# Cross-attention and a LoRA feed-forward on one core: the opening, the first scores, the FFN weights and the router's product put in another order and width

## The reference

```
xn  = layernorm(x);  q = xn @ Wq;  k = ctx @ Wk;  v = ctx @ Wv
p   = softmax(q k^T / sqrt(128) + bias, masked)          # 64 x 64 for each batch and head
x1  = x + (p v) @ Wo
x2  = layernorm(x1)
logits = x2 @ router_W^T + router_b (15 columns); the 8 largest probabilities, summed by expert: w
out = x1 + x2 @ base_W^T + base_b + 2 * ((x2 @ A^T) * w) @ B^T     # A: 8 experts x 16 = 128 columns
```

## Time and profile before

| | |
|---|---|
| median of 3 runs | 798.69 us |
| the profiled execution: its time, its span | 798.68 us, 796.9 us |
| TensorE busy | 781.5 us, 98% of the span |
| VectorE, ScalarE, GpSimd busy | 577.1, 335.2, 188.7 us |
| DMA | 118.35 MB, mean 149 GB/s |
| chain that ended last | TensorE 92%, VectorE 4%, ScalarE 2%, issue 2%, DMA 1% |

### The profile page before, as it was taken

One profiled execution on the slowest core, in us unless ns is written; L12 is line 12 of the kernel. 1 busy time (PEld: TensorE's weight loads), 2 busy tenths in 40 slices (PEclk: granted clock), 3 DMA queues, 4 the chain that ended last, 5 costly groups with the idle time before them and its releaser, 6 DMA issues.

```text
span 796.9 us, 16335 instructions
## 1 busy us (share of the span) xinstructions
PE 781.5 (98%) x6366; PEld 653.6 (82%) x6366; DVE 577.1 (72%) x1047; ACT 335.2 (42%) x657; POOL 188.7 (24%) x203
## 2 busy tenths in 40 slices
PE   8899999999999999999999999999999999999998
PEld 7788888888888888778888888887888888888886
DVE  3894526247677666687987798778878888768974
ACT  4553525245555555453433244423433343314420
POOL 0052232114424434242211221222211221010200
PEclk9999999999999999999999999999999999999999
DMA  6436673234454546674563356435553555343002
GB/s 224 146 146 224 205 259 134 105 133 160 159 185 159 172 158 187 213 234 125 160 172 120 108 160 186 121 108 167 164 142 112 145 160 173 101 121 88 0 3 104
DMA packets 108074, 118.35 MB, mean 149 GB/s; under 512 B 44239, under 2 KB 77007, under 8 KB 107998
## 3 DMA queue, kind: packets, MB, share of 16 engines
q1 hardware_dynamic: 107998, 117.31, 47.0%
HBM read 81.64 MB, written 35.65 MB: 147 GB/s over the span
## 4 chain that ended last, share of the span: by engine, by line
PE 92%; DVE 4%; ACT 2%; issue 2%; DMA 1%; SPq 0%; DVEq 0%
PE pY L1378 40%; PE pP L1378 39%; PE pY L1540 4%; PE pO L1565 2%; PE pO L1378 1%; PE pT_ L1565 1%; PE pT_ L1550 1%; PE pS L1550 1%; DMA ctx<-in_ctx 1%; ACT wv_hi L646 1%; DVE y L1096 1%; DVE pr L1135 1%; PE pS L1565 1%; PE pO L1424 1%; DVE sm L1126 0%
## 5 line engine op out<-in xcount | busy, mean ns | idle before, releaser
L1096 DVE TENSOR_TENSOR y<-y,pY 128x512 f32<-128x512 f32 x124 | 84.5, 682 | 19.5 <-PE pY L1378 19.3
L1378 PE MATMUL pY<-wo_hi,oT_hi 128*128 128x512 f32 x248 | 97.2, 392 | 0.7 <-DVE y L1096 0.6
L1378 PE MATMUL pY<-wo_lo,oT_hi 128*128 128x512 f32 x248 | 96.6, 390 | 0.0
L1378 PE MATMUL pY<-wo_hi,oT_lo 128*128 128x512 f32 x248 | 96.5, 389 | 0.0
L1378 PE MATMUL pP<-xo_hi,wk_hi 128*128 128x512 f32 x210 | 83.4, 397 | 0.8 <-ACT v_s L631 0.8
L1378 PE MATMUL pP<-xo_hi,wk_lo 128*128 128x512 f32 x210 | 82.0, 390 | 0.5 <-issue 0.5
L646 ACT CAST wk_hi<-twk 128x256 fp32r<-128x256 f32 x128 | 52.1, 408 | 71.3 <-PE pP L1378 59.9
L1378 PE MATMUL pP<-xo_lo,wk_hi 128*128 128x512 f32 x210 | 81.9, 390 | 0.0
L579 POOL TENSOR_TENSOR bias<-bias,madd 128x512 f32<-128x512 f32 x32 | 43.9, 1382 | 150.3 <-DMA bias<-in_fside_Bx32xSxS 150.3
L885 DVE TENSOR_TENSOR wk_lo<-twk,wk_hi 128x256 fp32r<-128x256 f32 x128 | 58.7, 463 | 22.0 <-ACT wk_hi L646 22.0
L885 DVE TENSOR_TENSOR wk_lo<-wk_raw,wk_hi 128x256 fp32r<-128x256 f32 x96 | 45.7, 476 | 25.6 <-ACT wk_hi L646 25.4
(11 more groups left out here) (277 smaller groups left out, 1912.0 us busy)
## 6 DMA issues: line engine op xcount, KB each, us to landing
v_hbm<-stage SPq DMA_DIRECT2D x64, 256.0 KB, 2.2
k_hbm<-stage SPq DMA_DIRECT2D x64, 256.0 KB, 3.5
k<-k_hbm SPq DMA_DIRECT2D x16, 1024.0 KB, 5.4
v<-v_hbm SPq DMA_DIRECT2D x16, 1024.0 KB, 7.6
wk_raw<-in_L_xattn_Wk SPq DMA_DIRECT2D x16, 512.0 KB, 4.4
wo_raw<-in_L_xattn_Wo SPq DMA_DIRECT2D x16, 512.0 KB, 3.6
bias<-in_fside_Bx32xSxS SPq DMA_DIRECT2D x128, 64.0 KB, 3.5
wk_raw<-in_L_xattn_Wq SPq DMA_DIRECT2D x16, 512.0 KB, 4.6
```

The lines of the kernel that those rows point to most:

```text
L1096: nc.vector.tensor_tensor(y[:, t, :], y[:, t, :], src[:, :], ALU.add).then_inc(y_added, 1)
L1378: mm = nc.tensor.matmul(bank_, a, b, start=first and n == 0, stop=last and n == len(terms) - 1, skip_group_check=read_between)
```

## The change

Nothing is computed in another way; instructions move in the lists of TensorE, ScalarE and VectorE. `warm_up` has 22 transposes instead of 20. The router's product takes GW = 144 columns instead of ARW = 256; the tiles and the zeros in them stay. Hunks 1 and the last are the width; then, by position, ScalarE's opening (line 681), its block 32 (787) and its end (848), VectorE's opening (1008), its loop (1042), block 32 (1159) and end (1261), and TensorE's opening (1466), block 32 (1621), and end (1667).

```diff
@@ -23,6 +23,8 @@
 ARW = 256
+
+GW = 144
 SCALE = float(DH) ** -0.5
@@ -679,22 +681,22 @@
             higher(0, 1)
+            wait_raw(act, 0, (0, 1))
+            nc.scalar.copy(b12[0][:, :, :], raw_block(0, 0, 1)).then_inc(b12_h, 1)
+            higher(0, 5)
             last_high(0)
...
                            ).then_inc(a21_h, 1)
-            wait_raw(act, 0, (0, 1))
-            nc.scalar.copy(b12[0][:, :, :], raw_block(0, 0, 1)).then_inc(b12_h, 1)
             rows_out(1)
...
             copy_p1(1)
-            higher(0, 5)
+            higher(0, 3)
             sums_high(1)
             piece_of_first(2, 4, pP[1], c21_made)
-            higher(0, 3)
+            higher(0, 2)
             piece_of_first(1, 3, pP[0], c12_made)
-            higher(0, 2)
             piece_of_first(3, 7, pP[1], c22_made)
@@ -702,8 +704,8 @@
             copy_p1(2)
+            copy_v(1)
             sums_high(2)
-            copy_v(1)
             higher(0, 6)
@@ -787,10 +789,10 @@
             higher(w, 2)
-            exp(0)
             higher(w, 3)
...
             higher(w, 4)
+            exp(0)
             copy_c12(n)
@@ -848,13 +850,13 @@
             wo_high(NP - 1)
+            split_ffn(4)
             turned_p(h + 2)
             turned_p(h + 3)
-            split_ffn(4)
             split_ffn(5)
+            split_ffn(6)
             o_high(h + 2)
             o_high(h + 3)
-            split_ffn(6)
 
@@ -1008,23 +1010,23 @@
 
+            first_low(0)
             lower_w(0, 0)
-            first_low(0)
             first_low(1)
             lower_w(0, 1)
+            dve.wait_ge(b12_h, 1)
+            lower(b12[1][:, :, :], raw_block(0, 0, 1), b12[0][:, :, :], b12_l)
+            first_t3()
 
...
                   a21_l)
-            dve.wait_ge(b12_h, 1)
-            lower(b12[1][:, :, :], raw_block(0, 0, 1), b12[0][:, :, :], b12_l)
+            first_t2()
+            lower_w(0, 5)
             sums_of_a(1)
-            lower_w(0, 5)
+            lower_w(0, 3)
             sums_low(1)
-            first_t3()
-            first_t2()
-            lower_w(0, 3)
             lower_w(0, 2)
@@ -1042,11 +1044,14 @@
                 w, late, j = next_set(n), late_set(n), prep_at(n)
+                if n < NV:
+                    make_c11(n)
                 if w is not None:
...
                     lower_w(late, 5)
-                make_c11(n)
+                if n >= NV:
+                    make_c11(n)
                 if w is not None:
@@ -1159,23 +1164,23 @@
             lower_w(late, 6)
+            lower_w(w, 2)
+            lower_w(w, 3)
             biased(0)
-            lower_w(w, 2)
+            make_c22(n)
             largest(0)
...
             largest(1)
-            lower_w(w, 3)
             less_max(1)
-            make_c22(n)
             lower_w(w, 4)
-            add_up(0)
             lower_w(w, 5)
...
             n, w2 = QA + 1, next_set(QA + 1)
+            add_up(0)
+            lower_w(w, 6)
             weights(0)
-            lower_w(w, 6)
             lower_w(w2, 0)
@@ -1261,14 +1266,14 @@
             add_tile(i, 6)
+            split_ffn(4)
             add_tile(i, 7)
...
             o_low(h + 2, 1)
-            split_ffn(4)
-            split_ffn(5)
             o_low(h + 3, 0)
             o_low(h + 3, 1)
+            split_ffn(5)
             split_ffn(6)
@@ -1466,9 +1471,8 @@
             turn_ctx(0, first_turn(0))
-            warm_up(4)
+            warm_up(14)
             turn_ctx(1, first_turn(1))
-            warm_up(8)
 
@@ -1621,11 +1625,12 @@
             times(n - 1, 4)
-            times(n, 6)
+            for p in (6, 7, 5):
+                times(n, p)
             scores(0)
             scores(1)
-            for p in (7, 5, 3, 4):
-                times(n, p)
+            times(n, 3)
+            times(n, 4)
             for p in (1, 2, 6, 7, 5, 3, 4):
@@ -1667,13 +1672,14 @@
                 times_wo(i, t)
+                if t == 5:
+                    ffn_weights(4)
             turn_p(h + 2)
             turn_p(h + 3)
-            ffn_weights(4)
             ffn_weights(5)
+            ffn_weights(6)
             times_v(h + 2)
             times_v(h + 3)
-            ffn_weights(6)
 
@@ -1690,8 +1696,8 @@
                     pe.wait_ge(sel_made, E + 1)
-                product(pG[t // 2][:, t % 2 * ARW:(t % 2 + 1) * ARW],
-                        [(xt, (ar[0][:, c, :], ar[1][:, c, :])) for c, xt in enumerate(xt_parts(t))]
+                product(pG[t // 2][:, t % 2 * ARW:t % 2 * ARW + GW],
+                        [(xt, (ar[0][:, c, 0:GW], ar[1][:, c, 0:GW])) for c, xt in enumerate(xt_parts(t))]
                         ).then_inc(g_full, 1)
...
             def base(t):

```

## The result

The changed kernel took **797.17 us** (median of 20 runs, 795.54 to 799.17) against 799.53 us for the kernel before on the same chip (20 runs, 797.39 to 804.88): ratio 0.9968, 95% interval [0.9955, 0.9981], 2.6 us less. Forecast were 794.3 us and 4.4 us less. The profiled executions don't show this: the one after took 799.1 us (span 797.3), the second slowest of its 20, and the one before 798.68 (span 796.9), the seventh fastest of its 20.

A forecast was written before the change was run, and what follows sets the result against it. TensorE, busy 781.5 of 796.9 us, was taken as the bound. Opening -2.7, first scores +0.3, FFN weights -1.0 and router's width -1.0 sum to -4.4: 798.7 to 794.3 us, range 791.2 to 797.5.

The forecast's parts named there:

- The start: TensorE's opening: 14 transposes before context tile 1's turn bring the first product from 9.51 to about 8.5 us, -1.0 us.
- the end of -1.7: Opening: the start's saving if unbroken transposes bring the clock's rise before the first product, instead of -1.0 us.
- B12, B22, T3: Opening: work moved into VectorE's idle time and ScalarE's list ends TensorE's waits at 26.93 and 20.89 us, -1.3 us.
- `copy_v` and the sums: Opening: `copy_v(1)` first shortens the `v_s` wait, -0.7 us; the sums' low part slips, new wait +0.8 us.
- The cover of A21: Opening: A21 ready about 15.2 us, wanted at 15.6, a thin margin; a wait at 15.5 would show the forecast wrong.
- `make_c11`: Opening, VectorE: placed ahead of `lower_w(w, 0)`, the piece no longer stands behind a held-up low part, -0.5 us.
- First scores: Block 32, scores behind product 5: `v_s` wait hidden, -0.93; later pieces +0.8 and +0.5; sum +0.3 us, -0.9 to +0.9.
- FFN weights: End: batch 4 turned after tile 5 ends the `fw_lo` wait, last Wo starts at about 738.05, -1.0 us (-0.3 to -1.3).
- The router's width: Router: 96 matmuls at 144 columns take 0.11 instead of 0.12 us each, -1.0 us.
- The nearest row: Router: transposes of 128 columns, each with its weight load, 0.11 us apart, taken as the narrow matmul's price.
- Rival 1: Router: narrow fp32r product is slow, up to 0.28 us per matmul, +15 us; total 800 to 810 us; chance 0.15.
- Rival 2: VectorE, nearly full in the opening and around 335 to 345 us, takes back TensorE's gain; 796.5 us, chance 0.25.

The follow-up runs named there:

- e3: Kernel before with only batch 4 of the FFN weights turned and split earlier; 797.53 us, ratio 0.9977.
- e4: Kernel before with only the router's product at 144 columns; 799.83 us, ratio 1.0005.
- e14: Changed kernel with 4 transposes instead of 14 between the turns of context tiles 0 and 1; one run, 803.69 us.
- e6: Kernel before with GpSimd's mask addition cut to one element per partition, keys not masked; 796.46 us, ratio 0.9966.
- e9: Changed kernel with copy_c12(32) ahead of exp(0) on ScalarE and add_up(0) behind make_c11(33) on VectorE; 796.79 us, ratio 0.9954.
- e10: Changed kernel with block 32's three stores and a weight load between the two halves of the bias loads in SP's queue; 796.62 us, ratio 0.9960.
- e15: Changed kernel with e9, e10 and add_tile(i, 0) ahead of add_up(h + 3) on VectorE together; 796.04 us, ratio 0.9947.
- e5: Changed kernel with block 32 as before on all three engines, so without the moved scores; 795.27 us, ratio 0.9948.
- e11: Changed kernel with block 32 as before and add_tile(i, 0) ahead of add_up(h + 3) on VectorE; 795.44 us, ratio 0.9947.
- e7: Changed kernel with GpSimd's mask addition cut to one element per partition, keys not masked; 793.72 us, ratio 0.9926.

## Why the forecast was right or wrong

The time fell by 2.6 us where 4.4 were forecast. (The 798.7 from which the forecast subtracts was the median of three runs, 0.8 us below that of twenty.) The same distances in all profiles of these runs, by the old and the new version of each part (mean, lowest to highest):

| stretch | old lists | new lists | forecast |
|---|---|---|---|
| start of the first product | 8.8 (7.7 to 10.1), 6 profiles | 7.7 (7.4 to 8.1), 10 | -1.0 |
| start of the 1345th matmul of 512 columns | 326.1 (323.9 to 328.5), 5 | 322.5 (322.1 to 323.2), 10 | -2.7 |
| from there over the scores to 356 us | 32.23 (32.0 to 32.5), 7 | 33.75 (33.2 to 34.1), 7 | +0.3 |
| attention loop, masks in, `add_up` first | 356.1 (354.4 to 357.1), 4 | 356.7 (355.1 to 358.8), 8 | 0 |
| loop's end to the router (before, e3) | 37.04 | 36.10 | -1.0 |
| router to 787 us (before, e4) | 36.95 | 36.41 | -1.0 |

Their sum is -3.7 + 1.5 + 0.6 - 0.9 - 0.5 = -3.0 us, beside the -2.6 of the ratio. The start stands in the second row too. The ranges of the first scores' row do not touch; those of the loop's do, and its 0.6 can't be told from nothing. By luck the opening gave 1.0 more than its forecast and hid most of the 1.2 that the scores cost beyond theirs.

- **The start (-1.0).** The rise of the clock was assumed to keep its distance to the first product. It came before it: in the changed kernel's profile it is -1.64 at the first matmul of 512 columns and -2.06 at the seventh, near the end of -1.7 that the forecast had kept for this case. The rule of the Trainium skill (TensorE: Matmul & The Clock Gate, Part 4: PE-mode transpose) that transposes don't count is not borne out here: TensorE had done nothing but transposes, and the turn behind the 14 took 0.60 us instead of 1.11 and the first product ran at the high level. With four of them and standstills (e14) the level was lost again after three matmuls.
- **B12, B22, T3 (-1.3), `copy_v` and the sums (-0.7 + 0.8).** As forecast: no wait for `wv_lo` at 25 us; at 31.73 a wait of 0.77 for `v_s` and at 33.89 one of 0.54 behind the sums' low part, which ends at that time. The cover of A21 was as thin as said, and it often failed: in 8 of the 12 profiles with the new lists (not in the changed kernel's own) TensorE waits 0.25 to 0.48 us for it between 14.4 and 15.5 us, which the forecast had named as a sign of being wrong.
- **`make_c11` (-0.5).** -0.4 in the pair of profiles. It is worth more: in two of five profiles with the old order (e4, e6) the wait was 2.03 us, with the new order none was seen. By these rows this and the clock are what makes the opening's mean -3.7 and not the forecast's -2.7.
- **First scores (+0.3): the step that failed.** Its first half held: the wait for `v_s` went, and the two waits came where they were foreseen (`exp` ahead of `copy_c12`, `add_up` ahead of `make_c11`), 0.53 and 0.48 us. Block 32 and 33 take 23.95 instead of 23.36 us, +0.6, inside the forecast's bounds. What the sum lacked is the first pair behind them: from block 33's last product over turns, scores and V it takes 7.34 us on average (6.9 to 7.7) in the seven profiles without the moved scores and 8.31 (7.8 to 8.6) in the seven with them, e9, e10 and e15 left out. Half of the 0.97 stands ahead of the first product with V (0.52 on average), half behind it (0.45). Ahead: SP's queue and one piece of VectorE. Of the queue: eight bias loads, which start when the scores are read, take 5.22 us, the last store of block 32 goes out behind them at 340.04 (337.71 in e5), V's load waits for it, 345.92 instead of 343.10, and TensorE waits 0.2 to 1.0 us for V in six of the seven. The piece is `make_c21(33)`, for which the scores wait: they take 2.40 us, 2.08 before. Behind: the gap before TensorE's next instructions come, 1.0 to 1.3 us in those seven, 0.3 to 0.95 in the others. e10 took V's wait away and gained nothing, the gap was 1.59. Why the packet with the instructions starts later when the scores stand later stays open. The forecast counted the move on three engines, left out its DMAs, and stopped at block 33.
- **FFN weights (-1.0).** -0.94. Wo starts at 740.00, 0.10 after `o_low`; the profile files the wait of 1.12 under issue.
- **The router's width (-1.0).** -0.54. The nearest row, transposes at 0.11, was the right one. The 96 matmuls save 0.008 each, not 0.01, since 0.11 and 0.12 were rounded from 0.1115 and 0.1195; that makes 0.77 us, of which 0.54 arrive. The Trainium skill's 107 ns for a load of 128 columns (the same page, LDWEIGHTS) lies just under the floor of 0.1115. Rival 1 (a slow narrow mode) is out: no width from 144 to 240 is slower.
- **Rival 2** (VectorE takes back what TensorE gains, 796.5 us) came nearest in time, but not by its own steps: the opening kept its gain. It came true in the scores and perhaps, by some 0.6 us, in the loop, whose collisions with GpSimd the forecast did not look at.

## What to carry to other kernels

Follow a moved step past the block it was moved in, its DMAs and queue included: here two thirds of the cost lay in the next pair of heads. When VectorE is close behind TensorE, a repaired wait mostly makes the next in its list visible; e9, e10 and e11 each mended what they meant to and gained nothing that could be told. Where the table of waits says "issue", look at the packets of the instruction queue. And where one execution differs from the next by 3 us, judge an edit of 1 us by the stretch that it touches, over several profiles, not by one pair.

## What the runs showed that was not expected

- VectorE's steps with two SBUF operands take longer beside GpSimd's additions: 0.17 us became 1.27, 0.68 became 1.74, 1.22 became 3.42; the step `y<-y,pY`, with an operand in PSUM, kept its 0.68. The Trainium skill (SBUF — State Buffer, SBUF: two separate sides) says that the two share a port pair under an exclusive lock held for the whole instruction. The trace agrees: the low part that began at 46.36 ended at 49.78, 1.08 after GpSimd's sum. By it the order of the two lists is a matter of time, not only of dependences.
- Taking GpSimd's mask additions out of the attention loop is worth about 2.7 us to the kernel before and 3.4 to the changed one (e6, e7), as much as the whole change.
- Like standstills are followed by the low clock level in one execution and not in another: behind 2.03 us of waiting for the same piece the granted clock was 0.62 and 0.52 in e4 (50 to 54 us) and stayed 1.00 in e6 (53 to 57 us). In e14 it fell 0.8 us after a restart, and behind 1.12 us at 740.00 it stayed high in the profile after.
- TensorE stands still for 0.2 to 2.2 us, each time until shortly after a packet of instructions, among the small products with V, at like places in every profile, most of them some 78 us (three pairs of heads) apart, the longest in e14. The table of waits calls it "issue"; only the packets of the instruction queue show it.
- fp32r matmuls of 144 to 240 columns start every 0.112 us, of 256 every 0.1195, of 512 every 0.227.
